# Stick-breaking attention: the second exponential moved ahead of the next block's softplus on ScalarE, and issued once for two heads

## What is computed

```python
# 32 heads of 64, per head; i = query, j = key, strictly lower triangle
z   = einsum('bhid,bhjd->bhij', q, k) / sqrt(64)
mask = tril(ones(l, l), k=-1)
lom = where(mask, -softplus(z), 0)
s   = flip(cumsum(flip(lom, -1), -1), -1) - lom   # sum of lom over the keys behind j
att = where(mask, exp(log_sigmoid(z) + s), 0)
o   = einsum('bhij,bhjd->bhid', att, v)
```

## Time and profile before

| | us |
|---|---|
| median of 3 runs | 8151.83 (8098.16 to 8205.3) |
| the profiled execution, whole | 8178.73 |
| its span on the slowest core (core 2) | 8177.2 |
| spans of the 8 cores | 8083.6 to 8177.2 |
| TensorE busy | 5930.3 |
| ScalarE busy | 2887.1 |
| VectorE busy | 2682.1 |

### The profile page before, as it was taken

How to read it: one execution, slowest core, us unless ns; L and a number is a source line. 1 busy time by engine, 2 the same in 40 slices (tenths; PEclk the granted TensorE clock), 3 DMA queues, 4 the chain that set the end, 5 groups by cost and what they waited for, 6 DMA issues and landing times.

```text
span 8177.2 us, 80517 instructions; the slowest of 8 cores (8083.6 to 8177.2 us)
## 1 busy us (share of the span) xinstructions
PE 5930.3 (73%) x18740; PEld 1720.7 (21%) x18740; DVE 2682.1 (33%) x4660; ACT 2887.1 (35%) x4754; POOL 854.1 (10%) x1617
## 2 busy tenths in 40 slices
PE   2222668689999999999999765577677757766775
PEld 0101212122222222222222122111221212121112
DVE  7211222122222222222222110465066326614650
ACT  0000234245555544454555300354054215503440
POOL 0011201111111111111100000100200010011001
PEclk9866755666666666666665588787888888888878
DMA  2000458420000000000000144211611251143116
GB/s 73 16 6 9 51 63 89 55 28 9 7 8 8 8 8 8 8 7 7 8 4 1 30 101 85 63 57 34 195 54 57 91 143 53 53 129 106 53 37 177
DMA packets 222103, 408.76 MB, mean 50 GB/s; under 512 B 141576, under 2 KB 144032, under 8 KB 215760
## 3 DMA queue, kind: packets, MB, share of 16 engines
q0 software_dynamic: 200592, 353.00, 20.5%
q1 hardware_dynamic: 20784, 50.47, 2.6%
q10 hardware_dynamic: 272, 0.14, 0.0%
HBM read 451.83 MB, written 85.07 MB: 66 GB/s over the span
## 4 chain that ended last, share of the span: by engine, by line
PE 49%; DMA 19%; DVE 12%; issue 9%; ACT 5%; another core or an unknown queue 4%; DVEq 1%; SPq 0%; ACTq 0%; POOL 0%; POOLq 0%
PE pbq L510 7%; PE zp L631 5%; PE zp L625 5%; DMA cd<-scr_cd 5%; PE pbL L637 5%; DVE gu L818 4%; DMA xp<-x 4%; PE zp L548 3%; PE pboA L572 3%; PE pboB L572 3%; ACT g L810 2%; DMA wk<-WkT 2%; DMA wv<-WvT 2%; PE pbL L807 2%
## 5 line engine op out<-in xcount | busy, mean ns | idle before, releaser
L642 DVE TENSOR_TENSOR lsb<-lsb,pbL 1x512 bf16<-1x512 bf16 (+3 forms) x1152 | 674.9, 586 | 1572.4 <-PE pbL L637 1557.0
L566 ACT ACTIVATE att<-zp 128x512 bf16<-128x512 f32 (+3 forms) x1280 | 640.0, 524 | 541.5 <-PE zp L631 535.4
L599 ACT ACTIVATE texp<-zp 128x1024 bf16<-128x1024 f32 x448 | 458.5, 1023 | 881.5 <-PE zp L548 684.8
L625 PE MATMUL zp<-sp,tri 128*128 128x512 bf16 (+3 forms) x1280 | 652.7, 510 | 5.9 <-ACT sp L611 5.9
L631 PE MATMUL zp<-lsb,ones 1*128 1x512 bf16 (+2 forms) x1152 | 611.2, 531 | 0.0
L637 PE MATMUL pbL<-sp,negones 128*1 128x512 bf16 (+3 forms) x1152 | 558.5, 485 | 53.8 <-DVE lsb L642 53.1
L790 ACT ACTIVATE zg<-zp 128x512 bf16<-128x512 f32 x64 | 38.2, 597 | 1464.1 <-PE zp L787 1464.1
L818 DVE TENSOR_TENSOR gu<-g,pbL 128x512 bf16<-128x512 bf16 x704 | 483.7, 687 | 189.4 <-PE pboB L804 65.4
L818 DVE TENSOR_TENSOR gu<-g,zp 128x512 bf16<-128x512 bf16 x704 | 483.6, 687 | 167.4 <-ACT g L810 54.3
L810 ACT ACTIVATE g<-zp 128x512 bf16<-128x512 f32 x704 | 420.3, 597 | 277.3 <-PE zp L804 204.4
L810 ACT ACTIVATE g<-pboB 128x512 bf16<-128x512 f32 x704 | 420.3, 597 | 231.3 <-PE pboB L804 151.0
(11 more groups left out here) (186 smaller groups left out, 6857.7 us busy)
## 6 DMA issues: line engine op xcount, KB each, us to landing
cd<-scr_cd POOLq DMA_DIRECT2D x256, 512.0 KB, 4.7
cgu<-scr_cgu POOLq DMA_DIRECT2D x136, 704.0 KB, 4.7
scr_cgu<-CguT POOLq DMA_DIRECT2D x32, 704.0 KB, 80.4
x<-x SPq DMA_DIRECT2D x16, 1024.0 KB, 4.8
scr_cd<-CdT POOLq DMA_DIRECT2D x32, 512.0 KB, 78.2
xp<-x SPq DMA_DIRECT2D x64, 256.0 KB, 4.8
out<-op SPq DMA_DIRECT2D x64, 256.0 KB, 3.2
out<-yst POOLq DMA_DIRECT2D x16, 1024.0 KB, 8.0
```

The source lines that it names most:

```text
L566: Sc.op("ACT", lambda sc, zp=zp, hs=hs, c0=c0: sc.activation(t_att[zp][:, 512 * hs + c0:512 * hs + 512], zpair_ap[zp][:, 512 * hs + c0:512 ...
L625: Sc.op("PE", lambda t, zp=zp, h0=h0, c0=c0, pz=pz: t.matmul(zpair_ap[zp][:, h0 + c0:h0 + QT], t_tri[:], t_sp[zp][:, h0 + c0:h0 + QT], sta ...
L642: Sc.op("DVE", lambda v, hs=hs, c0=c0: v.tensor_tensor(t_lsb[hs][:, c0:QT], t_lsb[hs][:, c0:QT], pbank[2][0:1, c0:QT], op=ALU.add), reads= ...
```

## The change

In `emit_att_o` the two ScalarE instructions for `att` become one over both heads (1024 columns) where the step is full width; in a narrow step they stay two. In either case both now stand ahead of both products with v, and the tile has one name, `att0` or `att1`, in place of one for each head: each product with v waits for both halves. The call of `emit_att_o(pend)` moves from behind the first `yield` of a step to ahead of the step's own `texp` and `sp`. So ScalarE's order in a step goes from texp(jb), sp(jb), att(jb+1) to att(jb+1), texp(jb), sp(jb). On TensorE the order of the attention's own matmuls does not change; a unit of `gen_qkv` at the first `yield` of a step stood between the products of L637 and those of L572, and now stands between those of L572 and those of L548. No arithmetic is added or left out.

```diff
@@ emit_att_o
+            if c0 == 0:
+                Sc.op("ACT", lambda sc, zp=zp: sc.activation(
+                    t_att[zp][:], zpair_ap[zp][:], AF.Exp),
+                    reads=[pr[(0 if zp == 0 else 6)], pr[(0 if zp == 0 else 6) + 1]],
+                    writes=[res(f"att{zp}")])
+            else:
+                for hs in range(2):
+                    Sc.op("ACT", lambda sc, zp=zp, hs=hs, c0=c0: sc.activation(
+                        t_att[zp][:, 512 * hs + c0:512 * hs + 512],
+                        zpair_ap[zp][:, 512 * hs + c0:512 * hs + 512], AF.Exp),
+                        reads=[pr[(0 if zp == 0 else 6) + hs]], writes=[res(f"att{zp}")])
             oc0 = 0 if first else c0
             for hs in range(2):
-                Sc.op("ACT", ... t_att half hs ..., writes=[res(f"att{zp}h{hs}")])
                 ...
-                    reads=[rvtok, res(f"att{zp}h{hs}")], writes=[pr[po]])
+                    reads=[rvtok, res(f"att{zp}")], writes=[pr[po]])
@@ gen_headpair, memset of the att tile of the first step
-                        writes=[res(f"att{fzp}h{hs}")])
+                        writes=[res(f"att{fzp}")])
@@ gen_headpair, loop over jb
                 c0 = 128 * max(Dd, 0)
+                if pend is not None:
+                    emit_att_o(pend, qt, jbmax)
                 if c0 == 0:
                     Sc.op("ACT", ... texp ...)
                 ...
                 yield
-                if pend is not None:
-                    emit_att_o(pend, qt, jbmax)
                 if jb > 0:
                     emit_z(jb - 1, qt, 0)
                     emit_z(jb - 1, qt, 1)
```

## The result

| | before | after |
|---|---|---|
| median of 10 runs, us | 8169.6 (8098.2 to 8230.6) | 8608.0 (8559.8 to 8675.3) |
| ratio | | 1.056, 95% interval 1.050 to 1.062 |
| profiled execution, span, us | 8177.2 (core 2) | 8665.2 (core 1) |
| end of the attention (start of its last copy of pboA) on core 5, us | 4620.0 | 5079.7 |

The kernel is 5.6% slower. The forecast was 8600 us, and 446 us more in the attention. What comes behind the attention is about as long as before on every core (3470 to 3560 us before, 3470 to 3520 after). The fastest runs of both kernels stand 462 us apart, the medians 438.

The account below looks back on a forecast made before the run. TensorE's own queue bounds the attention. Head pairs 0 and 1 add nothing, head pair 2 at most 11, twelve more 396, the last 39: +446 us on 8178.7 gives 8625, median 27 lower, 8600; range 8500 to 8690.

Parts of the forecast that it names:

- What bounds the kernel before: Attention: bound by TensorE's own queue, 10.00 of 10 us busy at clock 0.50; ScalarE, 6.24 of 10, has slack.
- The full-width step, 4.72 to 6.09: Attention step without a unit between: TensorE waits for att, then for sp; +1.37 us a step.
- closed chain: Full-width step: last ones product, then att, texp, sp, then the next triangle product; 3.35 us from ones to triangle product.
- The first narrow step, -0.67: First to second step of a query tile, 4.05 us: att runs right behind the triangle products, saving 0.67.
- The second transition: Second to third step of a query tile: att, then four instructions of 384 columns; 4.35 to 4.55, +0.20.
- Where a unit lies between: Projection units, 3.63 us, hide the chain they stand in; uncovered gaps and tile's end in second query tile cost 2.4.
- What is hidden: First three head-pair boundaries: weight waits absorb the delay; head pairs 0 and 1 cost nothing, head pair 2 at most 11.
- A: Full-width steps: only the wait for att counts, 0.8 a step, not 1.37; sum 260, time 8410; 5 in 100.
- B: Attention: TensorE gets the higher clock where it now pauses; +0.27 a step, near 8245 us, +1.1%; 4 in 100.
- C: Interleaved stretch loses its clock through new pauses: 40 us a head pair, 480 more, 9080 us; 4 in 100.
- D: Not slower: TensorE stays the bound in full-width steps, only gains are left; near 8090 us; 2 in 100.
- The rule on merged instructions: Merged att on ScalarE: 186 ns + 0.833 ns a column, about 93 ns overlap; 1.04 us for 1024 columns.

Follow-up runs that it names:

- the kernel with pairs: Kernel before, with three pairs of matmuls laid out to run beside each other and both triangle products first: 8007 us, ratio 0.981.
- the two halves apart: Order alone in the kernel before: 8434 us, ratio 1.031; merge alone, the changed kernel with the call put back: 8446 us, ratio 1.034.
- the extra matmul: One full-size matmul with unread result behind the triangle group of full-width steps: kernel before 8114 and 8160 us, changed kernel 8609 us.
- the fastest kernels of the study: Paired matmuls, z products first, merged att behind texp and sp: 7857 us; the same with units at every fifth yield: 7823 us; both ratio 0.959.

## Why the prediction was right, point by point

- **What bounds the kernel before.** Right for the full-width steps at 1.2 GHz: with one more matmul they are 5.26 long. But the loop through ScalarE, 4.58 in the kernel with pairs, was nearly as long as TensorE's 4.72; the prediction spoke of slack and didn't say how little there was.
- **The full-width step, 4.72 to 6.09.** Measured 6.04. Both waits were forecast: 0.8 and 0.55, measured 0.75 and 0.49. The term 1.37 measured 1.32; the prediction rightly made it a closed chain, and the two halves apart and the extra matmul bear that out.
- **The first narrow step, -0.67.** This step failed. The prediction let `att` start right behind the triangle products. The timeline at the start of a fourth query tile, to be set beside the earlier trace rows:

```profile
2487.25 0.27 PE L632 MATMUL zp<-sp,tri 128*128 128x128 bf16 x1 [0.16 <-ACT sp L620]
...
2488.55 0.65 ACT L571 ACTIVATE att<-zp 128x128 bf16<-128x128 f32 x2 [1.45 <-DVE att L594]
...
2489.34 0.61 PE L579 MATMUL pboA<-att,vtok 128*64 128x512 bf16 x1 [0.34 <-ACT att L571]
...
2491.47 0.42 PE L632 MATMUL zp<-sp,tri 128*128 128x256 bf16 x1
...
2496.04 0.48 PE L632 MATMUL zp<-sp,tri 128*128 128x384 bf16 x1
```

  `att` had to wait for VectorE, which clears the unused columns of the same tile (L594) behind two copies and two clearings. Before, the four instructions of texp and sp had hidden that. 2491.47 - 2487.25 = 4.22, +0.17 in place of -0.67. The second transition, 4.57, was forecast with 4.55. In the fourth query tile the two errors nearly cancel: 18.0 + 0.84 for this step, less 12 x 0.05 for the full ones, makes 18.2, against 18.3 measured. That is luck, and it helps the whole: 13 x 0.84 too little, 13 x 20 x 0.05 too much. The third query tile took 13.6 more, forecast 13.0.
- **Where a unit lies between.** 2.4 us were forecast for the second query tile. On cores 2 to 7 it takes 62 to 65 us in most head pairs against 59 to 61: right. On cores 0 and 1 of the profiled execution it takes 68 to 75 in fifteen of twenty-two. Windows of that stretch on core 1, and of the same stretch on core 5:

```profile
2354.00:2360.00 6.00, 5.61 (x24) 2.11 (x22) 1.42 (x3) 2.69 (x6) 1.06 (x2) 0.81 0.17 16
```

```profile
2342.00:2360.00 18.00, 16.75 (x72) 6.18 (x71) 4.78 (x7) 5.99 (x6) 3.69 (x7) 1.00 0.14 13
```

  The clock there was 0.81 and not 1.00, and 16 products of a unit take 4.38 us there and 3.63 on core 5. So 0.81 is a level of its own here; the section on the profile before takes every value between 1.00 and 0.50 for a mixture of the two, and that is not so for this one. Single head pairs of the kernel before show such long tiles too (core 4, 71.5 for 61), four among the steady ones of its eight cores; no run tests whether the change makes them more frequent. The fastest runs of both kernels stand 462 apart and the medians 438, and core 5, which has no such tile after the change, lost 460, so the measured difference doesn't need them. The Trainium skill (TensorE: Matmul & The Clock Gate, section "Seeing it yourself", its note on the peak-current limiter) gives 13/16, that is 0.81, as the rate to which a die is held while three of its cores run dense matmuls; the value agrees, and no run here shows that this is the cause.
- **What is hidden.** The waits for weights at the first boundary of core 5, before and after:

```profile
PE pbq L510 <- DMA wq<-WqT: 31.4, 1, 31.4
```

```profile
PE pbq L510 <- DMA wq<-WqT: 4.7, 1, 4.7
```

  The wait took up 27 of the 33 us of delay. Not all was hidden: at the end of the fourth head pair core 5 is 58 us behind, where the prediction has 11 + 33 = 44 (its 33.5 - 22.5 should read 33.0 - 22.5). The weights of the second boundary on core 5, before and after:

```profile
1552.94 3.57 PE L510 MATMUL pbq<-xnF,wv 128*128 128x512 bf16 x8 [17.24 <-DMA wv<-WvT]
```

```profile
1566.96 1.44 PE L510 MATMUL pbq<-xnF,wv 128*128 128x512 bf16 x3 [22.52 <-DMA wv<-WvT]
```

  TensorE waits for wv in both kernels, and wv is there 14.0 us later; at the first boundary wq, wk and wv came 6, 9 and 12 later. These make up nearly all of the 14: the third head pair ends 46 behind on core 5, where the prediction has 33. On core 2, whose rows the prediction used, the same wv came at 1555.8 before and 1552.8 after; there the third head pair ends 33.4 behind (33 forecast) and the fourth 38. Over the eight cores the fourth ends 29 to 64 behind. So the term was nearly right where the transfers kept their times, and the premise that they do held on some cores only; why they came later on others stays open. From there on eleven head pairs add 33 each on core 5 in the mean (33.0 forecast; 24 in one, whose second tile took 69 in the kernel before, and 32 to 36 in the rest), and the last 41 (39.3).
- **The rivals.** A (no wait for sp) fell with the 0.49 in the timeline. B (a higher clock by pauses) fell: the fourth query tile of the changed kernel stays at 0.50, and the clock rose in it only in kernels that had full-size products or projection units put into it. C (clock lost through pauses) didn't come with the units where they were: 1.00 in the window on core 5 above, and a second query tile only 2.6 us longer. D asked whether TensorE's own work exceeds the chain; the extra matmul in the changed kernel shows that it does not.
- **The rule on merged instructions.** The forecast estimate of 1.04 us for 1024 columns by the Trainium skill (ScalarE: Activation LUTs, section "What ACT_TABLE_LOAD costs") stands beside 1.02 measured.

## What to carry to other kernels

An engine that works in order is a place where two chains meet: before moving an instruction ahead in its queue, ask what it waits for, and what behind it was ready. Here an instruction that waits for TensorE went ahead of two that did not, and a chain through a ScalarE that is busy a third of the time became the bound. Merging two instructions saves 0.12 us, and costs what the first half had been early: 0.79 a step with the old order, and 0.44 on top of the new one. In the kernel with pairs ScalarE did not wait for the second half's input, and there the merge stood in the fastest kernels of the study.

## What the runs showed of the hardware that was not expected

- The granted clock didn't follow TensorE's busy share. A step of ten products, two of 128x128x512 and eight smaller ones (64 or 1 rows of input, or 64 or 1 columns of output), had 0.50 at 10.00 of 10 us busy. One product of 128x128x512 more in each step brought 1.00 in part of the steps, two more a mean of 0.78 over 1900 to 4600 us against 0.63. In the longer step of the changed kernel one more left the clock at 0.50, and two more brought 0.77. Adding work whose result nobody read made the kernel before 0.8% faster (0.4 to 1.3).
- Two products with one row of input each, on partitions 0 and 32, take 0.61 us together, and two with one column of output each 0.59, what one takes alone.
- The hand-over times hardly changed between the kernels: 0.09 to 0.10 us from the last ones product's end to ScalarE (0.15 where the two run as a pair), 0.14 to 0.15 from ScalarE's end to TensorE. From the last ones product over three ScalarE instructions to the next triangle product it was 3.33 us at 1.2 GHz and 3.32 at 2.4 GHz (3.38 with pairs).
